# First batch's layer norm written straight into split operands; the other batches' norm as tiles inside the attention

## The reference, cut to what matters

```python
x = x + attn(layernorm(x), W_qkv, W_out)            # 16 heads of 64, rotary embedding, causal
x = x + memory_attn(layernorm(x), ctx, Wq, Wk, ...) # a recurrence over 64 context tokens, 16 heads of 32
x = x + experts(layernorm(x), router, ...)          # top 2 of 8 experts
```

## Time and profile before

| | us |
|---|---|
| median of 3 runs | 3173.12 |
| lowest, highest | 3170.09, 3174.43 |
| the profiled execution, device time | 3173.92 |
| its span, first to last instruction | 3172.4 |
| first instruction of the attention | 124.13 |
| its first projection (PE) | 149.24 |
| first row maximum (unit 0, DVE) | 182.80 |

### The profile page before, as it was taken

The page is one execution under the profiler, slowest core; times in us unless marked ns, Lnnn a source line. Parts: engine busy times, 40 slices in busy tenths (PEclk is TensorE's granted clock), DMA queues, the critical chain, the costliest instruction groups (busy, mean ns, idle before and its releaser), DMA issues. The chain is left out here.

```text
span 3172.4 us, 49736 instructions
## 1 busy us (share of the span) xinstructions
PE 2761.7 (87%) x15885; PEld 2295.6 (72%) x15885; DVE 1996.5 (63%) x3903; ACT 1695.8 (53%) x3244; POOL 1430.9 (45%) x1457
## 2 busy tenths in 40 slices
PE   4399998999989999899998487888874999999998
PEld 2288886888868888688887365767663888888886
DVE  5356665666666666666666367767764565566565
ACT  2256665666656666566666232322322667666765
POOL 1155454555546455455555134344432444444443
PEclk8599999999999999999999799999986999999999
DMA  6743343434443343434434444345424444444432
GB/s 180 169 106 91 86 104 90 104 85 98 93 101 92 85 105 91 109 79 97 94 71 95 114 102 125 112 112 132 115 86 148 93 93 102 96 93 95 98 59 47
DMA packets 224822, 320.96 MB, mean 101 GB/s; under 512 B 75968, under 2 KB 142528, under 8 KB 221312
## 3 DMA queue, kind: packets, MB, share of 16 engines
q1 hardware_dynamic: 177056, 205.52, 27.8%
q0 software_dynamic: 47584, 113.19, 14.2%
HBM read 243.37 MB, written 77.27 MB: 101 GB/s over the span
## 5 line engine op out<-in xcount | busy, mean ns | idle before, releaser
L930 ACT ACTIVATE a_pt<-a_PT 128x512 fp32r<-128x512 f32 (+3 forms) x768 | 350.4, 490 | 550.9 <-PE a_PT L820 550.3
L990 DVE TENSOR_REDUCE a_nmax<-a_S 128x1 f32<-128x1024 f32 (+7 forms) x512 | 385.4, 753 | 266.4 <-PE a_S L809 266.4
L999 DVE TENSOR_TENSOR a_pt<-a_PT,a_pt 128x512 fp32r<-128x512 f32 (+3 forms) x768 | 401.6, 550 | 233.2 <-ACT a_pt L930 232.3
L837 PE MATMUL a_O<-a_pt,a_v 128*128 128x256 f32 (+1 forms) x2560 | 355.6, 286 | 53.2 <-DVE a_ot L1014 53.2
L919 ACT ACTIVATE a_pb<-a_S,a_nmax 128x1024 f32<-128x1024 f32 (+7 forms) x512 | 380.3, 743 | 13.9 <-DVE a_nmax L990 13.7
L837 PEld LDWEIGHTS a_O<-a_pt,a_v 128*128 128x128 f32 x2560 | 323.4, 192 | 72.9 <-DVE a_ot L1014 68.4
L820 PE MATMUL a_PT<-a_ident,a_pb 128*128 128x128 f32 x2304 | 343.5, 276 | 32.1 <-DVE a_pt L999 29.0
L1878 DVE TENSOR_TENSOR e_w<-e_raw,e_w 128x1024 fp32r<-128x1024 f32 x238 | 280.9, 1219 | 122.1 <-ACT e_w L1828 121.9
L820 PEld LDWEIGHTS a_PT<-a_ident,a_pb 128*128 128x128 f32 x2304 | 272.1, 142 | 77.3 <-issue 35.2
L760 PE MATMUL a_Z<-a_xT,a_wq 128*128 128x512 f32 x512 | 242.4, 474 | 67.2 <-POOL a_wq L683 34.1
L708 POOL TENSOR_TENSOR a_rot<-a_tmp,a_rot 128x512 fp32r<-128x512 f32 x128 | 162.6, 1293 | 258.0 <-ACT a_rot L902 257.6
(11 more groups left out here) (266 smaller groups left out, 6992.2 us busy)
## 6 DMA issues: line engine op xcount, KB each, us to landing
a_qs<-a_rot SPq DMA_DIRECT2D x256, 128.0 KB, 2.3
a_kh<-a_rot SPq DMA_DIRECT2D x256, 128.0 KB, 2.3
a_kl<-a_rot SPq DMA_DIRECT2D x256, 128.0 KB, 2.3
e_rows<-scr_hs SPq DMA_DIRECT2D x40, 516.0 KB
a_raw<-in_wqk POOLq DMA_DIRECT2D x32, 512.0 KB, 3.8
scr_attT<-a_ot SPq DMA_DIRECT2D x256, 64.0 KB, 2.1
m_att<-scr_attT SPq DMA_DIRECT2D x32, 512.0 KB, 4.2
m_rb<-scr_rinv SPq DMA_DIRECT2D x64, 256.0 KB, 8.9
```

The source lines that it names most:

```text
L837: mm = pe.matmul(O[:, c0:2 * P], v2[:, n % 2, kt, h, :, :].rearrange("p a d -> p (a d)"), pt[j % 2][:, part, kt, c0:2 * P], start=kt == 0 ...
L930: act.activation(pt[u % 2][:, 0, 4 * s:4 * s + m, (qt % 2) * P:(qt % 2 + 1) * P], PT[(k + s) % 2][:, 0:m * P].rearrange("p (k q) -> p k q" ...
L990: dve.tensor_reduce(nmax[:, u % GU:u % GU + 1], S[u % 2][:, 0:cols], AXX, ALU.max, negate=True).then_inc(s_nb, 1)
L999: dve.tensor_tensor(pt[u % 2][:, 1, 4 * s:4 * s + m, q], PT[(k + s) % 2][:, 0:m * P].rearrange("p (k q) -> p k q", k=m), pt[u % 2][:, 0, 4 ...
```

## The change

Batch 0 alone is normalised in the context stage. ACT writes the high part and DVE the low part directly from PSUM to buffers that outlive the stage (`early`: x, first `wq`, first `wv`); the first weights are loaded and split there too, by ACT and POOL. The gates are transposed by PE, so that `scr_ba` has a row for each head. The attention starts with its constants and goes on to the first projection. SP issues the 32 loads of the recurrence behind the first two sets of score operands (`stack(0)`, `stack(1)`), and POOL waits for them in unit 9 (`context_start`).

Batches 1 to 3 are normalised as 8 tiles for each batch, in the 128 units before it, started in units w = 3, 15, 27, 39, 51, 63, 75 and 87 of these: POOL issues the load of the tile (w), DVE takes statistics (w + 2), POOL computes 1/sqrt by a power and one Newton step in six operations on one column, then normalises (w + 3), PE transposes two pieces into the free half of `a_O`'s bank (w + 5) and two more (w + 9), DVE copies each pair to `a_xs`, and SP stores (w + 10). The rotation's second product goes to one shared buffer (`part`) instead of a fourth of `tmp`, with a wait for POOL's additions.

```diff
 def context_phase(nc, io, dram, scan, early):
+            gp.dma_start(raw[:, 0, :], io["wqk"][0]).then_inc(s_raw[0], 16)
+            gp.dma_start(raw[:, 1, :], io["wv"][0]).then_inc(s_raw[1], 16)
...
+                act.activation(xT[:, 0, :, t * P:(t + 1) * P],
+                               pX[t % 2][:, :].rearrange("p (e t) -> p e t", e=ET), ACT.Copy).then_inc(s_xhi, 1)
...
-            with pe.Fori(1, B) as b:
-                norm_batch(b)
+            for c in range(CT):
+                pe.wait_ge(s_g3, c + 1)
+                pe.wait_ge(s_trc, c + 1)
+                pe.transpose(pT[c][0:2 * XH, 0:P], gt[:, c, :], ident[:, :]).then_inc(s_gT, 1)
...
+            def low(t):
+                dve.wait_ge(s_xhi, t + 1)
+                cols = slice(t * P, (t + 1) * P)
+                dve.tensor_tensor(xT[:, 1, :, cols], pX[t % 2][:, :].rearrange("p (e t) -> p e t", e=ET),
+                                  xT[:, 0, :, cols].bitcast(F32), ALU.subtract).then_inc(s_xlo, 1)
...
 def attention_phase(nc, io, dram, scan, early):
+        TILES = (3, 15, 27, 39, 51, 63, 75, 87)
+        def tile_in(u, lag):
+            b, w = (u - lag) // (GU * G), (u - lag) % (GU * G)
+            if u >= lag and w in TILES and b + 1 < B:
+                return b * QT + TILES.index(w)
+            return None
...
-        pieces = [("x", 0, e) for e in range(ET)] + [("wq", 0), ("wv", 0), ("wq", 1)]
+        pieces = [("wq", 1)]
...
+            def fetch_tile(m):
+                if m:
+                    gp.wait_ge(s_xt, 2 * m)
+                gp.dma_start(xt[:, :], io["x"][T + m * P:T + (m + 1) * P, :]).then_inc(s_x, 16)
+            def norm_tile(m):
+                gp.wait_ge(s_mv, m + 1)
+                rs.step(gp.tensor_scalar(nw[:, 0:1], mv[:, 1:2], EPS, None, ALU.add))
+                rs.step(gp.tensor_tensor(nw[:, 1:2], nw[:, 0:1], nw[:, 4:5], ALU.pow))
+                rs.step(gp.tensor_tensor(nw[:, 2:3], nw[:, 1:2], nw[:, 1:2], ALU.mult))
...
+                gp.tensor_scalar(xt[:, :], xt[:, :], mv[:, 0:1], nw[:, 3:4], ALU.subtract,
+                                 ALU.mult).then_inc(s_xn, 1)
...
                 for p in splits(u):
                     low(p)
+                if tile_in(u, 0) is not None:
+                    fetch_tile(tile_in(u, 0))
+                if tile_in(u, 3) is not None:
+                    norm_tile(tile_in(u, 3))
+                if u == 9:
+                    context_start()
...
+            def turn_tile(u, m, a):
+                if m + a:
+                    pe.wait_ge(s_xs, 2 * m + a)
+                pe.wait_ge(s_xn, m + 1)
+                if values_done(u):
+                    pe.wait_ge(s_ofree, values_done(u))
+                for k in range(2):
+                    mm = pe.transpose(O[:, (2 + k) * P:(3 + k) * P],
+                                      xt[:, (2 * a + k) * P:(2 * a + k + 1) * P], ident[:, :])
+                mm.then_inc(s_xt, 1)
...
+            def tile_stats(m):
+                dve.wait_ge(s_x, 16 * (m + 1))
+                dve.bn_stats(bst[:, :], xt[:, :]).then_inc(s_bn, 1)
...
                 if values_turn(u - 1) is not None:
                     out_add(values_turn(u - 1))
+                if tile_in(u, 2) is not None:
+                    tile_stats(tile_in(u, 2))
```

More of the change, by code:

```diff
@@ L175, in context_phase @@
         s_x = [rm.sem(f"x{i}") for i in range(2)]
+        s_raw = [rm.sem(f"raw{i}") for i in range(2)]
+        s_whi = rm.sem("whi")
+        s_wlo = rm.sem("wlo")
         s_bn = rm.sem("bn")
@@ L264, in _ @@
-            for half in range(2):
-                load(0, half)
-            with gp.Fori(0, B - 1) as b:
-                batch(b, True)
-            batch(B - 1, False)
-            for half in range(2):
-                gp.wait_ge(s_xst[half], 16 * B)
+            gp.dma_start(raw[:, 0, :], io["wqk"][0]).then_inc(s_raw[0], 16)
+            gp.dma_start(raw[:, 1, :], io["wv"][0]).then_inc(s_raw[1], 16)
+            for i, w in enumerate((wq, wv)):
+                gp.wait_ge(s_whi, i + 1)
+                gp.tensor_tensor(w[:, 1, :, :].rearrange("p e n -> p (e n)"), raw[:, i, :],
+                                 w[:, 0, :, :].rearrange("p e n -> p (e n)").bitcast(F32),
+                                 ALU.subtract).then_inc(s_wlo, 1)
@@ L298, in _ @@
                                ACT.Copy).then_inc(s_trc, 1)
+            for i, w in enumerate((wq, wv)):
+                act.wait_ge(s_raw[i], 16)
+                act.activation(w[:, 0, :, :].rearrange("p e n -> p (e n)"), raw[:, i, :],
+                               ACT.Copy).then_inc(s_whi, 1)
             for c in range(CT):
@@ new lines, in low @@
+            def low(t):
[3 more added lines that the diff above has]
+                                  xT[:, 0, :, cols].bitcast(F32), ALU.subtract).then_inc(s_xlo, 1)
+            stats(0)
+            for t in range(QT):
+                if t + 1 < QT:
+                    stats(t + 1)
+                normalise(t)
+                if t:
+                    low(t - 1)
@@ L374, in _ @@
+            low(QT - 1)
+            dve.wait_ge(s_xn, QT)
             dve.wait_ge(s_in, n_in)
@@ L713, in _ @@
                 rope_low(0, c)
-            low(pieces[6])
+            low(pieces[0])
             ch = Chain(gp, s_sc)
@@ L869, in _ @@
                     pe.transpose(zbank(("s", b, 0))[:, 0:P], rsum[:, b % 2, :], ident[:, :]).then_inc(s_zfull, 1)
+                for a in range(2):
+                    if tile_in(u, 5 + 4 * a) is not None:
+                        turn_tile(u, tile_in(u, 5 + 4 * a), a)
                 fill(u, 0)
@@ L874, in _ @@
                 if values_turn(u) is not None:
+                    for a in range(2):
+                        for lag in range(1, 4):
+                            if tile_in(u, 5 + 4 * a + lag) is not None:
+                                pe.wait_ge(s_xs, 2 * tile_in(u, 5 + 4 * a + lag) + a + 1)
                     values(values_turn(u))
@@ L936, in out_low @@
                 act.activation(otmp[:, :], O[HD:P, 0:2 * P], ACT.Copy).then_inc(s_otmp, 1)
-            for p in pieces[0:6]:
-                high(p)
             for c in range(2):
                 rope_high(0, c)
-            high(pieces[6])
+            high(pieces[0])
             for j in range(4):
@@ L1026, in _ @@
                     out_add(values_turn(u - 1))
+                if tile_in(u, 2) is not None:
+                    tile_stats(tile_in(u, 2))
+                for a in range(2):
+                    if tile_in(u, 5 + 4 * a) is not None:
+                        tile_out(tile_in(u, 5 + 4 * a), a)
                 for i, j in ends(q_steps(u - 1), 4):
```

266 lines of the change are left out of this document (139 added, 127 removed).

## The result

The changed kernel takes 3182.88 us (median of 7 runs, 3181.87 to 3184.67), the kernel before 3173.12 (7 runs, 3167.84 to 3180.16). The ratio is 1.0034, with a 95% interval of 1.0023 to 1.0046: slower by a third of a per cent, where 16.5 us less were forecast. The profiled execution took 3181.87 us, its span is 3180.1 against 3172.4.

What follows compares the result with a forecast made beforehand. PE was taken to bound the attention's steady part, with no projection in the first 149.24 us. Gain 80.5 less 64 back (10 + 5 + 29 + 12 + 6 + 2): 16.5 us less, 3156.6 against 3173.12; range 3119 to 3192.

Steps and rivals of the forecast that it cites:

- The start: Stretch before the attention's first projection: moves from 149.2 to 68.7 us, a gain of 80.5, bounds 77 and 83.
- The late load in units 41 and 89: Tile load queued behind POOL's raw load makes DVE wait: 4.8 us late, six times, 29 us, bounds 0 and 37.
- the rival that hides the tiles: Attention: neither the late loads nor their clock cost anything; 3122 us, chance 0.14.
- The norm in unit 68: POOL's 3.1 us normalising chain keeps PE standing 4.0 us, once a batch: 12 us, bounds 6 and 30.
- The chain's own rival: POOL's normalising chain takes 7 us, not 3.1, and adds PE waits in units 8, 20, 56: 3195 us, chance 0.14.
- The clock: PE's clock falls at a third of the nine new gaps, with 2 us lost each: 6 us.
- The rival that has it fall at every gap and come back soon: PE's clock falls at all nine gaps, 2 us each: 18 us in place of 6, 3169 us, chance 0.13.
- the longer half clock: Rival: half clock lasts as in the earlier trace, some 6 us a gap, 54 for 6: 3205 us, chance 0.05.
- The first tile: Attention's start: the recurrence's loads cost 2 us, 0 to 8, for unit 9 and the first tile.
- PE's transposes and DVE's copies: 24 tiles in the attention: 10 us for PE (7 to 26) and 5 for DVE (0 to 12).
- the likeliest case: The forecast itself: 3156.6 us, range 3140 to 3172, chance 0.54, of which 0.46 faster by more than 0.2%.

Runs made afterwards that it cites:

- e4: The changed kernel without tile work in the attention: norm of batches 1 to 3 left out, projections read raw x; 3101.74 us.
- e10: e6 plus 31 unread matmuls ahead of PE's wait for DVE's low part in units 42 and 90, six times; 3159.78 us.
- e3: The changed kernel with POOL's tile load at the head of the unit and its norm ahead of the weight's low part; 3117.51 us.
- e1: The changed kernel with POOL issuing the tile's load ahead of the unit's rotation additions and low parts; 3142.53 us.
- e6: The changed kernel with 36 matmuls whose results nobody reads ahead of PE's wait for the tile in unit 68, three times; 3168.48 us.
- e8: The changed kernel with the tile's load ahead of the next raw weight's load, but still behind the weight's low part; 3163.38 us.
- e5: e3 with SP issuing the recurrence's 32 loads ahead of the first two stacks of keys; 3108.68 us.
- e7: e3 with DVE copying each turned half tile out of PSUM twice; 3124.23 us, one run.
- e9: e3 with PE transposing each half tile twice into the same place; 3129.00 us, one run.
- e0: The changed kernel run again without edits, on a chip where the kernel before takes 3171.18 us; 3177.46 us.

## Why the prediction was wrong

**The start** was mis-sized to the good side. Gates end at 54.45 and not 58.0, the attention begins at 57.75 and not 61.8, its first projection at 64.89 and not 68.7. x landed 3.6 us earlier, not 1.5, and from there to tile 7's last step it is 17.1 us against 14.5 before (24.78 - 7.67, and 25.79 - 11.29 in the earlier trace rows): the low parts added 2.6 and not 4.1. So tile 7 and the gates are 1.0 us earlier than before and not 2.6 later. The gain is 84.35 us at the first projection and 82.55 at unit 0's row maximum, against 80.5; what takes the 1.8 between them was not looked into. e4 shows that it is kept through the attention, but for the 5.7 us that it has there.

**The late load in units 41 and 89** was right in place, cause and size. 4.8 us each was forecast; DVE waited 6.42 where 6.1 was reckoned, PE stood 4.49, and with the clock's share taken out (e10) a place costs 4.34 to 4.60, some 0.3 of it the tile's own work (e3). e1 shows that POOL's order is the cause. Of the rival that hides the tiles nothing is left.

**The norm in unit 68** was right in place and short in size: 4.0 forecast, 5.7 with the clock taken out (e6), 5.0 of it the wait and 0.7 the tile's own work (e3). The chain has 4.2 us and not 3.1; 0.8 of the 1.1 is the normalising operation, which I had priced at half of a subtraction with two operands for twice the columns, and 0.3 the power. The chain's own rival (slower from 5.2 to 5.7 us on) was not what made the kernel slower.

**The clock** is the step that failed: "a third of them with 2 us lost: 6 us". It fell at all nine, and behind a gap of 3.08 us at the first tile; the price of one fall was right (1.9 to 2.0 us by e6 and e10), the number was not: 17.7 us against 6. The rival that has it fall at every gap and come back soon had this right, at 3169 us with the other terms as forecast. The trace of the kernel before already spoke against a third. Its attention has six gaps of PE of 3.7 to 5.1 us (units 106, 108, 234, 236, 362 and 364), and the clock was low behind every one; of its three of 2.13 us two dropped it (rows under e8). It also answers the longer half clock that the forecast read from the earlier trace rows: a second gap of PE, of 4.37 us, ends at 511.86, inside the stretch from 510 to 515, so the low clock there is not the first gap's alone. The Trainium skill says in "TensorE: Matmul & The Clock Gate", section on HAM oscillation, that an engine that waits between bursts is throttled again, with the warm-up paid each time; the nine rows agree, and I had given that rule less weight than one gap of 5.02 us in the earlier trace rows deserved.

**The first tile** got 2 us with the recurrence's loads and cost 6.4, that is the wait for its load, the clock behind it and its own work; the load ran beside the recurrence's 32 loads on SP and reached DVE in 6.6 us (117.99 less 111.40). Without them beside it 4.1 us go (e5).

**PE's transposes and DVE's copies** got 15. All else than the ten places measured 16.7, of which 5.5 stand in e4 too, where there are no tiles. That leaves 11 for the tiles' work outside the ten places; with what stays in these places when the waits are gone (4.2 in e3's nine, some 0.7 for the first tile) it is 16 us, and 24 times e3's mean of 0.73 is 17.5: right in size. The split (10 for PE and 5 for DVE) is not borne out: doubled, the two add about the same (e7, e9). The four transposes in the context, 1.11 us, which the forecast took to be at 2.4 GHz, are for three of the four batches at the lower level (granted clock 0.50 from 70 to 80 us); they gave only an upper bound.

In sum, against 64 forecast. The nine places have 64.4 us, where 47 were forecast with their clock. Of these 17.4 more, 11.7 are the clock (17.7 for 6) and 5.2 the norm, 2.2 of which is the tiles' own work, forecast with the 15; the late loads, with such work in them too, took 2.5 less than forecast; and 3.0 are what the nine places cost more in this execution than in e0, 2.4 of it where the half clock lasted longer. Then come 4.4 by the first tile and 1.7 in the rest: 64 + 17.4 + 4.4 + 1.7 = 87.5. With 82.55 gained and 2.8 us more behind the attention the span is 7.7 us longer. The time after was inside the range given (3119 to 3192); the likeliest case's own range (3140 to 3172) was missed, and with it the sign. The net was a small difference of two sums four to five times its size: the clock alone would have left it at 3168 to 3171, near no change, and the norm and the first tile (9.6 more) turned the sign.

## What to carry to other kernels

When work is moved from a stage of its own into a dense stage, the cost is less its instructions (here 16 to 18 us for 24 tiles) than where its issue stands in each queue (here 65 us, which e3 took away): ask for data at the head of an iteration, ahead of whatever the engine may wait for, and put what another engine waits for ahead of what is wanted later. Two moves of a few lines turned 0.34% slower into 1.7% faster than before, and with the recurrence's loads moved it is 1.9% (e5, 3108.68 us; how much of the last step is this edit's, the totals don't say). A gap of TensorE in a dense stretch is priced as its length plus the fall of the clock behind it: in this kernel for every gap of 3 us and more, and for most of those of 2.1 to 2.4.

## What the runs showed of the hardware

- Nine gaps of 4.2 to 5.2 us in otherwise dense work each dropped the granted clock to 1.2 GHz, and it was back 4 to 8 us after the gap; with 31 or 36 matmuls more in the gap it stayed at 1.00 every time. Of six gaps of 2.23 to 2.41 us (e8) five dropped it, of 42 of 2.13 us 32, of 42 of 1.65 to 1.67 us none (14 profiled executions), and one of 3.08 us at the first tile did (0.50 from 120 to 124 us).
- POOL's tensor-scalar operation on 128x512 with two column operands took 2.09 us (24 times, 2.09 to 2.10), its addition of two tensors of that shape 1.27 to 1.29. The power on one column took 0.57, the other one-column operations 0.19 to 0.23.
- A load of 256 KB from POOL's queue landed in 2.9 to 3.1 us in units 39 and 87 with nothing right ahead of it (e8), in 4.0 to 4.3 with a raw load of 512 KB ahead (the changed kernel), and in 6.6 beside the loads on SP (7.9 in e0).
